# A third-layer similarity normalised by one factor tile for 16 batches, its squares summed four turns later from DRAM

## What is computed

```
L0, L2 (the same function):
    xn     = transpose(x)                       # 512 nodes, 64 batches, 128 features
    x_norm = xn / max(norm(xn over the 128 features), 1e-12)
    sim    = einsum('nbl,mbl->nm', x_norm, x_norm) / B
    A      = sim where it is among the 153 largest of its row (not itself), else 0
    out    = (D^-1/2 A D^-1/2) applied to x @ adj + bias
L1: two kernels of the nodes from h W_lang and h W_grav (cosine, and exp of minus
    the squared distance), masked and normalised by row, mixed, times h W_V W_O
L3: x mixed once more with adj*adj + identity
```

## Time and profile before

| | |
|---|---|
| time, median of 3 runs (lowest, highest) | 1570.79 us (1570.73, 1571.62) |
| the profiled execution: its time, its span | 1571.14 us, 1569.3 us |
| granted TensorE clock, mean over the span | 0.963 |
| PE, DVE, ACT, POOL busy | 93%, 76%, 56%, 34% |
| first similarity | 0 to 143 us |
| first adjacency | 147 to 285 us |
| middle stage, loop of 13 turns of 49.4 us | 334 to 977 us |
| turn `nearly` | 1026 to 1071 us |
| turn `last` with the third similarity | 1071 to 1195 us |
| second adjacency | 1198 to 1313 us |
| last layers | 1317 to 1569 us |

### The profile page before, as it was taken

One profiled execution on the slowest core, in us unless ns is written; L12 is line 12 of the kernel. 1 busy time (PEld: TensorE's weight loads), 2 busy tenths in 40 slices (PEclk: granted clock), 3 DMA queues, 4 the chain that ended last, 5 costly groups with the idle time before them and its releaser, 6 DMA issues. The chain is left out here.

```text
span 1569.3 us, 27466 instructions
## 1 busy us (share of the span) xinstructions
PE 1460.9 (93%) x7672; PEld 1233.4 (79%) x7672; DVE 1191.6 (76%) x3055; ACT 884.5 (56%) x1579; POOL 541.4 (34%) x746
## 2 busy tenths in 40 slices
PE   6998996899999999999999999999998945999996
PEld 6887975688888888888888888877887944777774
DVE  5996997466667766677667776667776996999997
ACT  5754653346554565545655466554444942777775
POOL 5950010113331233312332123320200001999996
PEclk9999997899999999999999999999998976999998
DMA  9803953202121122211212112032431000444443
GB/s 363 282 1 134 395 188 108 68 21 81 67 80 43 51 80 67 80 40 54 80 67 80 40 54 79 29 139 91 154 109 34 0 0 21 128 147 141 141 146 107
DMA packets 81473, 156.59 MB, mean 100 GB/s; under 512 B 8781, under 2 KB 8909, under 8 KB 81421
## 3 DMA queue, kind: packets, MB, share of 16 engines
q1 hardware_dynamic: 81420, 155.95, 29.2%
HBM read 105.45 MB, written 50.46 MB: 99 GB/s over the span
## 5 line engine op out<-in xcount | busy, mean ns | idle before, releaser
L835 POOL TENSOR_TENSOR rs_a<-ve_a,neghalf 128x1 f32<-128x1 f32 x64 | 35.1, 548 | 398.5 <-DVE nm_a L829 398.5
L1107 PE MATMUL bank<-wov,ht_hi 128*128 128x512 f32 x512 | 161.5, 397 | 0.4 <-DVE y_lo L1498 0.4
L1498 DVE TENSOR_TENSOR y_lo<-bank,y_hi 128x512 fp32r<-128x512 f32 x128 | 84.3, 688 | 94.5 <-ACT y_hi L1246 94.3
L254 PE MATMUL bank<-xn_lo,xn_hi 128*128 128x512 f32 (+1 forms) x640 | 148.9, 363 | 3.9 <-DVE xn_lo L231 3.5
L226 ACT ACTIVATE xn_hi<-xn 128x512 fp32r<-128x512 f32 x128 | 80.8, 631 | 116.8 <-DVE xn L219 104.0
L1246 ACT ACTIVATE y_hi<-bank 128x512 fp32r<-128x512 f32 x128 | 72.4, 590 | 117.7 <-PE bank L1080 113.2
L1309 ACT ACTIVATE xo<-xo,nb_b,rs_b 128x512 f32<-128x512 f32 x64 | 52.2, 815 | 132.6 <-POOL nb_b L837 132.6
L1934 POOL TENSOR_TENSOR xw_lo<-xres,xw_hi 128x512 fp32r<-128x512 f32 x64 | 82.8, 1295 | 126.8 <-ACT xw_hi L1895 126.8
L245 PEld LDWEIGHTS bank<-xn_hi 128*128 128x128 f32 x512 | 96.4, 193 | 18.9 <-ACT xn_hi L226 1.7
L1080 PE MATMUL bank<-ht_hi,u_lang 128*128 128x512 f32 x320 | 109.9, 392 | 0.1
L1061 PE MATMUL bank<-an_hi,xw_hi 128*128 128x512 f32 x256 | 103.6, 405 | 6.4 <-DVE xw_lo L1498 3.2
(11 more groups left out here) (236 smaller groups left out, 4320.8 us busy)
## 6 DMA issues: line engine op xcount, KB each, us to landing
xw_dram<-stage SPq DMA_DIRECT2D x64, 256.0 KB, 5.3
stage<-xw_dram SPq DMA_DIRECT2D x64, 256.0 KB, 2.8
stage<-in_x SPq DMA_DIRECT2D x64, 256.0 KB, 2.7
between<-xo SPq DMA_DIRECT2D x64, 256.0 KB, 2.0
xres<-between SPq DMA_DIRECT2D x32, 512.0 KB, 3.7
xin<-between SPq DMA_DIRECT2D x64, 256.0 KB, 2.7
out<-xo SPq DMA_DIRECT2D x64, 256.0 KB, 2.0
xr<-in_x SPq DMA_DIRECT2D x16, 512.0 KB, 8.8
```

The source lines that it names most:

```text
L254: mm = self.nc.tensor.matmul(out, h[:, c * P:(c + 1) * P], l[:, a:b], start=(i == 0 and c != 1), stop=False, skip_group_check=True)
L1107: mm = nc.tensor.matmul(yp[i % 2][:], ht[a][:, c, i, :], wov[b][:, c, :], start=(c == 0 and n == 0), stop=(c == CH - 1 and n == 2))
L1498: nc.vector.tensor_tensor(lo, full, hi.bitcast(F32), ALU.subtract).then_inc(done, 1)
```

## The change

The tiles of the third similarity are taken as in the first: 4 blocks of 16 batches, tile j of a block holding in partition p row 16p + j of the block's 2048 rows, so all 16 tiles have one factor tile (`factor_bank`, banks 6 and 7 in turn). 64 single spreads become 4 spreads of four 128x128 matmuls; the picking matmuls, the rounding of the squares and the rows in DRAM go.

The squares leave the turn's own chain. For each round of 4 tiles SP loads one transfer of 1 MB (`xt`) from the layer's output in DRAM, four turns behind; ACT squares the four tiles (`square_round`), POOL adds them into `acc` (`add_round`). Rounds 0 to 8 stand in the last 9 turns of the loop, round 9 in the turn after the loop, rounds 10 and 11 in `nearly`; the last 16 tiles are squared in `last`. Where a block starts (rounds 0, 4, 8) POOL has three additions instead of four. ACT, whose waits depend on the round, gets two loops of turns; POOL's and SP's turns are written out. In the second adjacency SP loads `x_at` from DRAM, and ACT only writes the products. `TAIL` gets new numbers.

```diff
-TAIL = {"scaled": 0, "k_sum": 1, "k_turned": 1, "kt": 3, "l1": [3, 7, 11, 15], "residual": [5, 9, 13, 17],
-        "stats": [6, 10, 14, 18], "norm": [8, 12, 16, 20], "square": [9, 13, 17, 21], "squares": 25, "sums_out": 27,
-        "root": 38, "cap": 39, "invert": [40, 43, 46, 49], "rows_hi": 50, "rows_lo": 51}
+TAIL = {"scaled": 0, "k_sum": 1, "k_turned": 1, "kt": 4, "l1": [3, 6, 9, 12], "residual": [5, 8, 11, 14],
+        "stats": [6, 9, 12, 15], "norm": [8, 11, 14, 17], "root_1": 8, "spread_1": 14, "sums_2": 17, "invert_2": 19,
+        "root_2": 20, "spread_2": 22, "squares_3": 22, "sums_3": 40, "invert_3": 42, "root_3": 43, "spread_3": 44}
@@ SP @@
+        def round_of_squares(r):
+            if r:
+                sp.wait_ge(squared, GRP * r)
+            if r % delay == 0:
+                for i in range(GRP):
+                    sp.wait_ge(stored[i], 16 * (r + delay + 1))
+            sp.dma_start(xt[:], block_rows(r // delay)[:, GRP * (r % delay):GRP * (r % delay + 1), :]).then_inc(xt_in, 16)
@@ PE @@
+            def block_sums(k):
+                pe.wait_ge(added, GRP + BLOCK * (k + 1))
...
+                for c in range(CH):
+                    mm = nc.tensor.matmul(at[:, c * BLOCK:(c + 1) * BLOCK], acc[:, k % 3, c * P:(c + 1) * P],
+                                          s.part_of[BLOCK][:], start=True, stop=True)
...
+            def spread(k):
+                pe.wait_ge(rooted, k + 1)
+                if k == 1:
                     pe.wait_ge(yb_ok, GRP + nb)
+                for c in range(CH):
+                    mm = nc.tensor.matmul(factor_bank(k)[:, c * P:(c + 1) * P], wide[:, c * P:(c + 1) * P], s.ident[:],
+                                          start=True, stop=True)
...
-            if C:
-                squares(0)
-                squares(1)
@@ ACT @@
+            def square_round(r):
+                act.wait_ge(xt_in, 16 * (r + 1))
+                for i in range(GRP):
+                    act.wait_ge(added, GRP * r + i + 1)
+                    nc.scalar.activation(sq[:, i, :], xt[:, i, :], ACT.Square).then_inc(squared, 1)
...
-            if C:
-                for i in range(GRP):
-                    square(i)
+            if rounds:
+                square_round(rounds[0])
...
             if B:
                 scale_l()
+            for r in rounds[1:]:
+                square_round(r)
+            if B:
                 v_hi(2)
...
-            if C:
-                sums_out()
@@ POOL @@
-            if gp is not None:
-                square_lo(0)
             root_a(3)
-            if gp is not None:
-                for i in range(1, GRP):
-                    square_lo(i)
+            for r in rounds[:1]:
+                add_round(r)
...
             if g is not None:
                 pool.wait_ge(q_ok, g + 1)
                 nc.gpsimd.tensor_tensor(r_l[:], q_l[:], s.neghalf[:], ALU.pow).then_inc(r_ok, 1)
+            for r in rounds[1:]:
+                add_round(r)
@@ second adjacency, ACT @@
-            with act.Fori(0, nb // 4 - 1) as q:
+            with act.Fori(0, nb // 4) as q:
                 for k in range(4):
                     take(4 * q + k, k)
-                    bring(4 * q + 4 + k, k)
```

More of the change, by code:

```diff
@@ L232, in low_part @@
                                      ALU.subtract).then_inc(self.lo_ready, 1)
-    def spread(self, pe, i, k, rows):
-        if i:
-            pe.wait_ge(self.normed, i)
-        self.nc.tensor.matmul(self.scale[:], selected(self.s, k), rows, start=True, stop=True).then_inc(self.scale_ready, 1)
     def squares(self, pe, i):
@@ L477, in first_similarity, with adjacency @@
     return engines
-def adjacency(nc, s, sb, sem, banks, weights, xres, early):
+def adjacency(nc, s, sb, sem, banks, weights, later, early):
     nb = s.nb
@@ L523, in adjacency @@
         x_at = s.place("x_at", PARTS, (4, N))
-        x_there, xw_made, xw_out = sem("x_there"), sem("xw_made"), sem("xw_out")
+        x, xres = later
+        x_there, xw_made, xw_out = [sem(f"x_there{k}") for k in range(4)], sem("xw_made"), sem("xw_out")
     an_lo_ok = sem("an_lo_ok")
@@ L530, in sync, with load @@
         def sync(sp):
-            pass
+            def load(b, k):
+                sp.dma_start(x_at[:, k, :], x[bass.ds(b, 1)].rearrange("a p n -> p (a n)")).then_inc(x_there[k], 16)
+            for k in range(4):
+                load(k, k)
+            with sp.Fori(0, nb // 4 - 1) as q:
+                for k in range(4):
+                    at = sp.snap(4 * q + 4 + k)
+                    sp.wait_ge(xw_made, 4 * q + k + 1)
+                    load(at, k)
     else:
@@ L964, in turn @@
                 elif kind == "store" and gp is not None:
+                    if i == 0 and r is not None:
+                        round_of_squares(r)
                     at = sp.snap(GRP * gp + i)
@@ L1150, in l1 @@
                 mm.then_inc(l1_made, 1)
-            def squares(half):
-                pe.wait_ge(sq_lo_ok, GRP * gp + 2 * half + 2)
-                if last and not half:
-                    pe.wait_ge(yb_ok, GRP + nb)
-                for i in (2 * half, 2 * half + 1):
-                    for n, part in enumerate((sq_hi, sq_lo)):
-                        mm = nc.tensor.matmul(tr[0 if last else 1][:], picked(s, i), part[:, i, :],
-                                              start=(i == 0 and n == 0), stop=(i == GRP - 1 and n == 1))
-                if half:
-                    mm.then_inc(n2_made, 1)
-            def spread(i):
-                pe.wait_ge(rows_ok[0 if i < known else 1], 1)
-                sums.spread(pe, i, i, rows[0 if i < known else 1][:])
+            def block_sums(k):
+                pe.wait_ge(added, GRP + BLOCK * (k + 1))
+                if k >= 2:
+                    pe.wait_ge(sums.normed, BLOCK * (k - 1))
+                at = sums_columns(k)
+                for c in range(CH):
+                    mm = nc.tensor.matmul(at[:, c * BLOCK:(c + 1) * BLOCK], acc[:, k % 3, c * P:(c + 1) * P],
+                                          s.part_of[BLOCK][:], start=True, stop=True)
+                mm.then_inc(n2_ok, 1)
+            def spread(k):
+                pe.wait_ge(rooted, k + 1)
+                if k == 1:
+                    pe.wait_ge(yb_ok, GRP + nb)
+                for c in range(CH):
+                    mm = nc.tensor.matmul(factor_bank(k)[:, c * P:(c + 1) * P], wide[:, c * P:(c + 1) * P], s.ident[:],
+                                          start=True, stop=True)
+                mm.then_inc(sums.scale_ready, 1)
             A, B, C = ga is not None, g is not None, gp is not None
@@ L1238, in turn @@
                 pe.wait_ge(tg_ok, g + 1)
-            if C:
-                squares(0)
-                squares(1)
-        turns(pe, turn)
+        turns_without_squares(pe, turn)
     def scalar(act):
         copy = lambda o, i: nc.scalar.activation(o, i, ACT.Copy)
-        def turn(gp, g, ga, following):
+        def turn(gp, g, ga, following, rounds):
             def ht_hi(i):
@@ L1384, in turn @@
                 y_hi(2)
+            if nearly:
+                root(0)
+                nc.scalar.activation(warm[:], s.inv_s2[:], ACT.Exp)
             if A:
@@ L1479, in turn @@
             keep(3)
[L1480 to L1488 removed]
+            root_a(3)
+            for r in rounds[:1]:
+                add_round(r)
+            if last:
+                for r in range((nb - BLOCK) // GRP, nb // GRP):
+                    add_round(r)
             if g is not None:
@@ L1678, in turn @@
                 kt_lo()
+            if nearly:
+                invert(0, 2)
             if A:
@@ L1751, in vector @@
         dve.sem_inc(yb_ok, GRP)
-        turns(dve, turn)
+        turns_without_squares(dve, turn)
     def first_roundings(act):
```

295 lines of the change are left out of this document (131 added, 164 removed).

## The result

| | before | after |
|---|---|---|
| median of the runs (lowest, highest) | 1571.20 us (1570.73, 1572.92), 4 runs | 1561.72 us (1560.20, 1562.21), 4 runs |
| the profiled execution: its time, its span | 1571.14, 1569.3 us | 1562.21, 1560.5 us |
| granted TensorE clock, mean over the span | 0.963 | 0.966 |

The account below looks back on a forecast made before the run. PE, busy 93% of the span, was taken as the bound. Terms -2.0 - 0.6 + 6.3 + 1.0 + 1.9 - 13.0 = -6.4 gave 1564.4 us against the median; own range 1559 to 1569, 8-in-10 range 1553 to 1575.

Parts of the forecast that it names:

- The turn without additions: Loop turns without a round: PE loses 1.87 us of matmuls but waits for `xw_lo`, gaining 0.50 a turn, -2.0 over four.
- The port: Loop turns: POOL's additions and DVE's diagonals exclude each other; +6.3 us over six four-addition turns, -0.6 over rounds 0, 4, 8.
- So 1.55 of the 1.6 reach `l0(0)`: Four-addition loop turns: nearly all of the diagonals' 1.6 us delay arrives at `l0(0)`, making the turn 1.05 us longer.
- The turn behind the loop: Round 9's turn: no gain from the removed matmuls, and some 1.0 of the 1.55 us delay comes through, +1.0.
- `nearly`: Turn `nearly`: `m` sooner, but round 11's squares delay `v_hi(2)` and the clamp waits; +1.9 us, between -1.2 and +3.5.
- 1.2 us sooner: In `nearly`, four squares alone take 2.1 us instead of 4.8, but `m` then waits for PE, so comes 1.2 us sooner.
- `last`: Turn `last`: batches without a spread take 1.57 us instead of 1.79, with smaller terms; -13.0 us, between -8 and -15.
- At most 0.1 us each: In `last`, the 20 small matmuls of two block sums and three spreads, at most 0.1 us each, +2.0 together.
- No collision at all: Loop: no addition holds up a diagonal, 1552.3 us; a variant within the rival given chance 0.30.
- the additions do not get in between: Loop: the fourth addition waits until the diagonals are through, or this operation does not contend; 1555.9 us, chance 0.30.
- The clock falls in the lengthened turns: Loop and start of `last`: waits drop PE's clock, losing 2.0 us in each of 7 turns and there; 1580.4 us, chance 0.13.
- `last` gives less: In `last`, DVE, slowed by additions and the denser rest of L1, becomes the bound; 1569.9 us, chance 0.10.

Follow-up runs that it names:

- the first experiment: Against the changed kernel, POOL makes the four additions behind `r_l` instead of ahead of it in turns with a round; 1554.2 us, ratio 0.9896.
- the fifth addition: Changed kernel plus a useless 128x512 addition behind the four in the turns of rounds 1, 2, 3, 5, 6 and 7; 1565.2 us, ratio 0.9966.

## Why the prediction was right, and where it was not

The mechanism was right: the gain is in `last`, the wait for `xw_lo` takes the place of the matmuls, and the additions hold up the diagonals. That the sum lies so near is in part luck. In the profiles the forecast has 6.4 us less and 8.9 came out; the loop was put 3.7 too high, `nearly` 0.8 too high, and 1.7 came behind `last` by the clock alone, while the gain in `last` was put 3.5 too high. Errors of 3.7, 0.8 and 1.7 us one way and 3.5 the other cancel in part.

**The turn without additions** was right to the hundredth: the wait of the earlier trace rows came back, 48.91 us.

**The port** was right in kind, and the runs show it: one order of POOL's list, moved alone, is worth 7.5 us. The term was mis-sized, +6.3 where 6 x (50.0 - 49.4) = +3.6 came out, and -0.6 where rounds 0, 4 and 8 gave -1.5. The step that failed is "So 1.55 of the 1.6 reach `l0(0)`": the two delays are 0.2 and 1.09, 1.3 and not 1.6, and 1.1 of them arrive. The first delay of 0.2 does not get there at all: `v_lo(2)` starts 43.99 us after the turn's `l0(0)` with three additions (574.23 - 530.24) and just so with no collision (720.28 - 676.29, in the first experiment). The slack was in the earlier trace rows: `v_hi(2)` starts 0.11 behind the end of `a_s` there, while two operations of ACT that only follow one another overlap in their rows by 0.1; so `v_hi(2)` waited for something else, 0.2 us, and I had taken the chain for the cause. The second delay falls on the third diagonal, not the second; it is 1.09 us, less than an addition's 1.3, and all of it arrives: 724.24 - 679.17 = 45.07, 1.08 later. With the slack and this size the three terms are 3.6 - 1.5 - 2.0 = +0.1, where the budget has 0.0.

**The turn behind the loop**, +1.0, was +1.1, and the additions moved behind `r_l` take 1.0 of it away again. The number is right by two errors: I had let 1.0 of 1.55 us come through, and all of a delay of 1.09 did.

**`nearly`** came to +1.1 (0.0 to the first squares, +1.1 to the first crosses), where I had +1.9. The squares have their +2.1 and the clamp +0.7 where I had 1.0. The piece that failed is "1.2 us sooner" for `m`: it comes 0.4 sooner on the clock of the span (1058.36 in the earlier trace rows, 1057.94 after) and `k_turned` 1.2 later (1028.96 and 1030.21), together 1.7. What I did not say is where the chain's delay lands: ahead of the first squares PE had the eight picking matmuls as a cover, and without them it is idle for 2.9 us.

**`last`** gained 9.5 from the first crosses on (the 1.1 ahead of them stand under `nearly`), not 13.0. The 1.57 us a batch is right, and so is what the additions do in it: remainders of 1.18 us, and DVE's lead falls by 2.0 us and covers it. "At most 0.1 us each" for the 20 small matmuls is the step that failed: they take 0.22 each, 0.88 for each set of four (eight rows of the trace, two for one matmul of the code), and a matmul of 16 columns (the sums) no less than one of 128 (the spread). That is 4.4 instead of 2.0 for the five sets; I had scaled a 512-column fp32r matmul down. With it the stretch from batch 16 on has -10.6 - 1.9 - 1.0 + 3.5 = -10.0, for -9.5 measured (one of the five sets falls before batch 16). The first 16 batches gained nothing where I had -1.5: the low clock at their start takes 1.5 us, which the experiment with the useless matmuls gives back.

**The second adjacency** is 1.7 us shorter, where I had 0; no change of work did that. In the profiled execution of before the clock fell behind the wait of 3.0 us at its start, in that of after it did not, and in four of the ten experiments, with nothing changed there, it did. So the 1.7 us belong to the two profiled executions and not to the change; how often the clock falls there in the other runs I do not know. The DMA loads of `x_at` cost nothing, as predicted: from DVE's first search to the end both take 364.8.

**The rivals.** *No collision at all* and *the additions do not get in between* fell, by the diagonal of 1.37 us. *The clock falls in the lengthened turns* fell: with waits of 0.67 and 1.16 in a turn it stays at 1.00 through the loop, also at 1.49 and 1.13 with the fifth addition; it fell in `last`, at 2.9 and 2.5. *`last` gives less* fell for this kernel. With four more additions and a later spread DVE did become the bound, 2.4 us, and the runs do not tell which of the two was needed.

## What to carry to other kernels

When work is taken off the busiest engine at one point, look for a place in the trace where that work is already missing: the turn ahead of the loop told the gain of a loop turn, 0.5 us where 1.9 us of matmuls went. Work that is moved to POOL has a price on DVE which is set by what DVE does at that moment: beside the diagonals, with both operands in SBUF, an addition cost up to 1.09 us, beside `v_lo`, `a_l` and `ht_lo`, which read PSUM, nothing. So its place in POOL's list is worth choosing, and here took the gain of the change from 9.5 to 17 us. An experiment that moves work should move nothing else: the one that also moved a spread left open which of the two cost the time. And before a delay is charged to the end, check what the waiting operation waits for in a turn without the delay; the first delay, taken at 0.3 us in each of nine turns, came to nothing at `l0(0)`, and these 2.7 us are most of the 3.7 that this forecast missed in the loop.

## What the runs showed that I had not expected

- An f32 matmul of 128x16 takes as long as one of 128x128: four of either put 0.88 us between the squares and the crosses of a batch.
- The clock's falls behind equal waits are not the same from one execution to the next: behind PE's wait of 3.0 us ahead of the second adjacency 5 profiles of 12 show it (granted clock 0.81 over that stretch in the one quoted, 1.00 in that of the changed kernel), at 1.3 to 1.7 us each time. A difference of 1.5 us between two profiled executions is no evidence for an edit; I needed the stretch in which it lies.
- Useless matmuls in PE's idle time kept the granted clock at the start of `last` at 1.00 instead of 0.50 and shortened the first 16 batches by 1.5 us in the profiled execution, while the medians stayed the same.
